# Two graph aggregations by Strassen's seven block products in a four-layer graph kernel on one core

## The reference

```python
x = _layernorm(x + _L0_gnn_ref(...))   # multi-head masked attention, 8 heads
x = _layernorm(x + relu(matmul(matmul(adj, x), W1.T) + b1))
x = _layernorm(x + _L2_gnn_ref(...))   # edge attention
a = adj + eye; d = sum(a, axis=1) ** -0.5
x = _layernorm(x + relu(matmul(d[:, None] * a * d[None, :] @ x, W3.T) + b3))
```

## Time and profile before

| what | us |
|---|---|
| median of 3 runs | 2519.9 (2518.26 to 2522.22) |
| the profiled execution: its own time | 2521.61 |
| the profiled execution: span of its instructions | 2519.8 |
| PE busy in the span | 2411.4 (96%) |
| layer 1: projection, then aggregation | 68.0, then 210.9 |
| layer 3: projection, then aggregation | 67.1, then 210.8 |

### The profile page before, as it was taken

The page is one execution under the profiler, slowest core; times in us unless marked ns, Lnnn a source line. Parts: engine busy times, 40 slices in busy tenths (PEclk is TensorE's granted clock), DMA queues, the critical chain, the costliest instruction groups (busy, mean ns, idle before and its releaser), DMA issues. The chain is left out here.

```text
span 2519.8 us, 66825 instructions
## 1 busy us (share of the span) xinstructions
PE 2411.4 (96%) x24900; PEld 1546.0 (61%) x24900; DVE 1546.1 (61%) x3013; ACT 1364.4 (54%) x2036; POOL 1146.4 (45%) x969
## 2 busy tenths in 40 slices
PE   7998999999999999999799997999999999979998
PEld 6886777777777777777544443774444545434443
DVE  4447888988988988888542223555545566532222
ACT  3337888888888888888533222225343444323221
POOL 0006888888888888888501232001111112310323
PEclk9999999999999999999999998999999999989999
DMA  4228999999999999999543664215668779743564
GB/s 160 67 67 153 191 183 187 195 180 189 195 181 186 195 178 187 194 174 187 103 146 137 213 201 145 90 42 156 172 177 194 194 215 226 167 134 103 207 215 141
DMA packets 783211, 417.40 MB, mean 166 GB/s; under 512 B 691248, under 2 KB 717488, under 8 KB 773936
## 3 DMA queue, kind: packets, MB, share of 16 engines
q1 hardware_dynamic: 783024, 414.62, 71.7%
HBM read 203.55 MB, written 40.84 MB: 97 GB/s over the span
## 5 line engine op out<-in xcount | busy, mean ns | idle before, releaser
L826 DVE CUSTOM_DVE_ANT_0 att_scores<-att_slots,l_bias 128x1024 f32<-128x1024 f32 x528 | 575.9, 1091 | 31.7 <-POOL att_part_low L651 14.2
L651 POOL TENSOR_TENSOR att_part_low<-att_scores,att_part_high 128x1024 f16<-128x1024 f32 x352 | 575.1, 1653 | 11.3 <-ACT att_part_high L810 0.6
L771 ACT ACTIVATE att_scores<-att_scores,att_nmax 128x1024 f32<-128x1024 f32 x528 | 552.4, 1047 | 18.1 <-DVE att_lifted L837 15.8
L692 PE MATMUL att_slots<-l_kk,l_q 128*128 128x512 f16 x2112 | 464.5, 355 | 7.4 <-POOL att_scores L631 4.4
L1365 PE MATMUL a_ps<-l_y,a_adj 128*128 128x512 f16 x1936 | 421.5, 381 | 9.0 <-DVE a_adj L1379 4.7
L780 ACT ACTIVATE att_near_high<-att_ps_t 128x512 f16<-128x512 f32 x528 | 258.2, 524 | 151.6 <-PE att_ps_t L702 138.9
L845 DVE TENSOR_TENSOR att_near_low<-att_ps_t,att_near_high 128x512 f16<-128x512 f32 x528 | 316.4, 599 | 38.5 <-ACT att_near_high L780 36.4
L1365 PEld LDWEIGHTS a_ps<-l_y,a_adj 128*128 128x128 f16 x1936 | 190.0, 98 | 240.5 <-DVE a_adj L1379 5.2
L692 PEld LDWEIGHTS att_slots<-l_kk,l_q 128*128 128x128 f16 x2112 | 194.8, 98 | 163.8 <-DVE att_least L826 20.9
L1110 PE MATMUL edge_ps_o<-l_sup,edge_pt_high 128*128 128x512 f16 x968 | 289.3, 381 | 2.2 <-DMA edge_pt_low<-edge_part_low 2.2
L1350 ACT ACTIVATE a_adj<-l_adj 128x2816 f16<-128x2816 f32 x44 | 112.0, 2549 | 291.0 <-DMA l_adj<-in_adj_cols 270.6
(11 more groups left out here) (157 smaller groups left out, 3836.9 us busy)
## 6 DMA issues: line engine op xcount, KB each, us to landing
l_adj<-in_adj_cols SPq DMA_DIRECT2D x44, 1408.0 KB, 6.1
l_adj_tiles<-in_adj SPq DMA_DIRECT2D x22, 1354.0 KB, 6.0
l_bias<-in_adj SPq DMA_DIRECT2D x63, 384.0 KB, 3.9
p_x_in<-x SPq DMA_DIRECT2D x66, 256.0 KB, 2.6
l_q<-q_rows SPq DMA_DIRECT2D x44, 256.0 KB, 3.9
a_xres<-x SPq DMA_DIRECT2D x44, 256.0 KB, 2.9
p_x_in<-in_x_cols SPq DMA_DIRECT2D x22, 256.0 KB, 2.6
q_rows<-l0w_q_halves SPq DMA_DIRECT2D x22, 256.0 KB, 2.0
```

The lines of the kernel that those rows point to most:

```text
L651: nc.gpsimd.tensor_tensor(out=part[1][:, v, lo:lo + width], in0=sc[:, v, lo:lo + width], in1=part[0][:, v, lo:lo + width], op=ALU.subtract ...
L692: mm = nc.tensor.matmul(slots[:, slot, z:z + w], q[:, u, h % 2, a, h // 2, :], kk[:, h, lo + z:lo + z + w], start=a == 0, stop=a == 1)
L771: nc.scalar.activation(sc[:, v, lo:lo + width], sc[:, v, lo:lo + width], ACT.Exp, bias=nmax[:, v:v + 1], scale=-1.0).then_inc(exp_done, 1)
L826: nc.vector.tensor_tensor_reduce(out=sc[:, v, lo:lo + width], in0=slots[:, (NC * h + c) % 2, 0:width], in1=adj[:, u, lo:lo + width], scale ...
```

## The change

Strassen's form splits adj Y into blocks: rows by odd and even tile of a pair (t = 2m + u), the sum over k by odd and even k, and the 512 columns of Y into two halves. Seven products of sums of blocks take the place of eight, each with 11 k-steps of 256 columns: 7 x 11 x 2 matmuls of 128x256 for a pair of tiles, where there were 2 x 22 x 2 of 128x512.

`project` (layers 1 and 3) now writes seven combinations of Y's blocks: ACT evicts each tile to fp32 (`y32`), and after each odd tile DVE makes five sums, ACT and DVE make the high and low parts of the two plain blocks and of the five sums. ACT narrows adj tiles 0 and 1 at tiles 6 and 10; then SP loads adj tiles 2 and 3; DVE makes the block sums of the first pair at tiles 12 to 15. The loops of `project` in these layers and of `aggregate` are written out.

`aggregate` works by pairs: ACT narrows three pairs deep, DVE makes five block sums of a pair ahead (`combine`), PE seven products, ACT copies four of them out, DVE adds them up in eight steps (`add`), and then bias, residual and statistics for each tile of the pair.

In layer 0 the first rows of adj come in four pieces, each ahead of one of the last four x loads.

```diff
+NARROW_AT = (6, 10)
+SUM_AT = 12
...
+def sum_blocks(nc, blocks, out, n, ready):
+    even, odd = [[blocks[:, u, e::2, :] for u in range(2)] for e in range(2)]
+    if n == 0:
+        for u in range(2):
+            op = nc.vector.tensor_tensor(out=out[:, u, :, :], in0=even[u], in1=odd[u], op=ALU.add)
+    else:
+        a, b, how = ((odd[0], odd[1], ALU.subtract), (even[1], even[0], ALU.subtract), (even[0], odd[1], ALU.add))[n - 1]
+        op = nc.vector.tensor_tensor(out=out[:, 1 + n, :, :], in0=a, in1=b, op=how)
+    op.then_inc(ready, 1)
...
             late(1, 1)
+            more = 0
             for dst, src in prefetch:
                 sp.dma_start(dst, src).then_inc(prefetched, 16)
-            if ahead is not None:
-                sp.dma_start(adj[:, 0, 0:N], adj_rows[0:P, :]).then_inc(first_adj, 16)
-            pairs(sp, 4, T, late)
+            quarters = 0 if ahead is None else len(ADJ_PARTS)
+            if warm is not None:
+                over(sp, 4, NARROW_AT[1] + 3, late)
+                sp.wait_ge(first_narrowed, 2)
+                for t in range(2, 4):
+                    sp.dma_start(a32[:, t % 2, :, :], columns_of(adj_cols, t)).then_inc(prefetched, 16)
+                    more += 1
+                over(sp, NARROW_AT[1] + 3, T, late)
+            else:
+                over(sp, 4, T - quarters, late)
+            for n in range(quarters):
+                lo, width = ADJ_PARTS[n]
+                sp.dma_start(adj[:, 0, lo:lo + width], adj_rows[0:P, lo:lo + width]).then_inc(first_adj, 16)
+                late((T - quarters + n) // 2, (T - quarters + n) % 2)
...
-                        pe.wait_ge(out_low, nj * (2 * m + u - 2) + n + 1)
+                        if combos is None:
+                            pe.wait_ge(out_low, nj * (2 * m + u - 2) + n + 1)
+                        else:
+                            pe.wait_ge(evicted, 2 * m + u - 1)
...
+            def halves(m, u):
+                t = 2 * m + u
+                act.wait_ge(made, t + 1)
+                if m > 1:
+                    act.wait_ge(out_low, 2 * m - 2)
+                scale = V_S * XW if row_scale is None else row_scale[:, bass.ds(t, 1)]
+                slots = y32[:, m % 2, 1::2, :] if u == 0 else y32[:, m % 2, 0::2, :]
+                if t in NARROW_AT:
+                    n = NARROW_AT.index(t)
+                    act.wait_ge(prefetched, 16 * len(prefetch))
+                    nc.scalar.activation(a16[:, 0, n, :, :], a32[:, n, :, :], ACT.Copy).then_inc(first_narrowed, 1)
+                nc.scalar.activation(slots, ps_job[0][:, u, :].rearrange("p (c n) -> p c n", c=2), ACT.Copy,
+                                     scale=scale).then_inc(evicted, 1)
+                if u == 1:
+                    act.wait_ge(evicted, t + 1)
+                    nc.scalar.activation(combos[0][:, 5:7, m, :], y32[:, m % 2, 1:3, :], ACT.Copy).then_inc(out_high, 1)
+                    act.wait_ge(y_summed, 3 * m + 3)
+                    nc.scalar.activation(combos[0][:, 0:5, m, :], sums[:, :, :], ACT.Copy).then_inc(out_high, 1)
...
+            def halves(m, u):
+                if 2 * m + u == SUM_AT:
+                    dve.wait_ge(first_narrowed, 2)
+                    if degrees is not None:
+                        add_identity(nc, a16[:, 0, :, :, :], 0, ident, first_summed)
+                        dve.wait_ge(first_summed, 2)
+                if 0 <= 2 * m + u - SUM_AT < 4:
+                    sum_blocks(nc, a16[:, 0, :, :, :], a_sum[:, 0, :, :, :], 2 * m + u - SUM_AT, first_summed)
+                if u == 0:
+                    return
+                dve.wait_ge(evicted, 2 * m + 2)
+                if m > 0:
+                    dve.wait_ge(out_low, 2 * m)
+                nc.vector.tensor_tensor(out=sums[:, 0:2, :], in0=y32[:, m % 2, 0:2, :], in1=y32[:, m % 2, 2:4, :], op=ALU.add) \
+                    .then_inc(y_summed, 1)
+                nc.vector.tensor_tensor(out=sums[:, 2:4, :], in0=y32[:, m % 2, 0:4:3, :], in1=y32[:, m % 2, 1:3, :],
+                                        op=ALU.subtract).then_inc(y_summed, 1)
+                nc.vector.tensor_tensor(out=sums[:, 4, :], in0=y32[:, m % 2, 1, :], in1=y32[:, m % 2, 2, :], op=ALU.add) \
+                    .then_inc(y_summed, 1)
+                dve.wait_ge(out_high, 2 * m + 1)
+                nc.vector.tensor_tensor(out=combos[1][:, 5:7, m, :], in0=y32[:, m % 2, 1:3, :], in1=combos[0][:, 5:7, m, :],
+                                        op=ALU.subtract).then_inc(out_low, 1)
+                dve.wait_ge(out_high, 2 * m + 2)
+                nc.vector.tensor_tensor(out=combos[1][:, 0:5, m, :], in0=sums[:, :, :], in1=combos[0][:, 0:5, m, :],
+                                        op=ALU.subtract).then_inc(out_low, 1)
...
+            def load_adj(t):
+                if t < T:
+                    sp.wait_ge(narrowed, t - 3)
+                    sp.dma_start(a32[:, t % 2, :, :], columns_of(adj_cols, t)).then_inc(adj_loaded[t % 2], 16)
...
+            for m in range(1, M):
+                load_adj(2 * m + 4)
+                load_adj(2 * m + 5)
+                for u in range(2):
+                    load_x(2 * m + u)
+                    norm.store(sp, out_rows, m - 1, u)
...
+            def narrow(m):
+                for u in range(2):
+                    if m > 1:
+                        act.wait_ge(adj_loaded[u], 16 * (m - 1))
+                    if m > 2:
+                        act.wait_ge(summed, PRODUCTS * (m - 2))
+                    nc.scalar.activation(a16[:, m % 3, u, :, :], a32[:, u, :, :], ACT.Copy).then_inc(narrowed, 1)
+            narrow(1)
+            narrow(2)
+            for m in range(M):
+                for n in range(2):
+                    act.wait_ge(summed, PRODUCTS * m + 2 + 4 * n)
+                    if m > 0:
+                        act.wait_ge(added, ADDS * m)
+                    nc.scalar.activation(copied[:, n, :, :], ps[:, m % 2, 2 * n, :, :], ACT.Copy) \
+                        .then_inc(copies, 1)
+                if m + 3 < M:
+                    narrow(m + 3)
 
...
-            def step(m, u):
-                t = 2 * m + u
-                pe.wait_ge(narrowed if dcol is None else diag_ready, t + 1)
-                if not (isinstance(m, int) and m == 0):
-                    pe.wait_ge(biased, t - 1)
-                for k in range(T):
-                    for b in range(2):
-                        mm = nc.tensor.matmul(ps[:, u, :], a16[:, u, k, :], y[b][:, k, :],
-                                              start=k == 0 and b == 0, stop=k == T - 1 and b == 1)
-                mm.then_inc(summed, 1)
-            step(0, 0)
-            step(0, 1)
-            pairs(pe, 2, T, step)
+            for m in range(M):
+                if m > 0:
+                    pe.wait_ge(combined, 4 * m)
+                if m > 1:
+                    pe.wait_ge(added, ADDS * (m - 1))
+                s16, s2 = a16[:, m % 3, :, :, :], a_sum[:, m % 2, :, :, :]
+                a11, a22 = s16[:, 0, 0::2, :], s16[:, 1, 1::2, :]
+                factors = [(s2[:, 4, :, :], 4), (a22, 2), (s2[:, 0, :, :], 6), (s2[:, 2, :, :], 0),
+                           (a11, 3), (s2[:, 1, :, :], 5), (s2[:, 3, :, :], 1)]
+                for n, (a, c) in enumerate(factors):
+                    for k in range(M):
+                        for b in range(2):
+                            mm = nc.tensor.matmul(ps[:, m % 2, n // 2, n % 2, :], a[:, k, :], y[b][:, c, k, :],
+                                                  start=k == 0 and b == 0, stop=k == M - 1 and b == 1)
+                    mm.then_inc(summed, 1)
 
...
+            def combine(m):
+                s16, out = a16[:, m % 3, :, :, :], a_sum[:, m % 2, :, :, :]
+                dve.wait_ge(narrowed, 2 * m)
+                if dcol is not None:
+                    add_identity(nc, s16, m, ident, diag_ready)
+                    dve.wait_ge(diag_ready, 2 * m)
+                if m > 1:
+                    dve.wait_ge(summed, PRODUCTS * (m - 1))
+                for n in range(4):
+                    sum_blocks(nc, s16, out, n, combined)
+            def add(m):
+                m5, m7, m6 = (ps[:, m % 2, n // 2, n % 2, :] for n in (2, 3, 6))
+                m1, m4, m3, m2 = (copied[:, n // 2, n % 2, :] for n in range(4))
+                c11, c12, c21, c22 = (total[:, n // 2, n % 2, :] for n in range(4))
+                if m > 0:
+                    dve.wait_ge(r_ready, 2 * m)
+                for n, (made, out, a, b, op, own) in enumerate((
+                        (2, c11, m1, m4, ALU.add, 0), (4, c11, c11, m5, ALU.subtract, 1), (4, c11, c11, m7, ALU.add, 2),
+                        (6, c12, m3, m5, ALU.add, 0), (6, c21, m2, m4, ALU.add, 0), (6, c22, m1, m2, ALU.subtract, 0),
+                        (6, c22, c22, m3, ALU.add, 6), (7, c22, c22, m6, ALU.add, 7))):
+                    dve.wait_ge(copies, 2 * m + (1 if made < 6 else 2))
```

(64 more changed lines are left out.)

89 lines of the change are left out of this document (35 added, 54 removed).

## The result

The changed kernel takes 2571.4 us (median of 4 runs, 2568.44 to 2572.69), where the kernel before took 2520.7 beside it: a ratio of 1.0199 (95% interval 1.0186 to 1.0213). It is 50.7 us slower, where 28.6 were forecast; the time lies inside the range given. The profiled execution took 2572.69 us, 51.1 more than that of before.

The account below looks back on a forecast made before the run. PE was taken to bound projections and aggregations. A layer: 33.4 projection + 1.2 front - 24.3 aggregation + 5.5 tail = +15.8; two layers +31.6, layer 0 -3.0: +28.6 us, 2548.5 us; 8-in-10 range 2526 to 2588.

Parts of the forecast that it names:

- The aggregation, -24.3 us a layer: PE in the aggregations: 1694 matmuls of 256 columns at 0.109 us replace 968 of 512, saving 24.3 us a layer.
- rival 2: Aggregations: DVE bounds them, with dear block sums and a POOL normalisation lost per pair; 2587 us, chance 0.09.
- the cheap end: DVE's block sums in the aggregations: about 0.9 us each instead of 1.64, DVE's total 12.8 us a pair instead of 16.5.
- Handover +1.2: Front of the aggregation: the projection's last chain is longer though tile 0's narrowing leaves the gap; 1.2 us more a layer.
- tail +5.5: End of the aggregation: two tiles leave PE at once, 11.3 us to the last normalisation instead of 5.8; 5.5 more a layer.
- layer 0 -3.0: Layer 0: adj rows loaded in four pieces let x 4 come in time, removing PE's idleness of 3.0 us.
- The chain, 2.46 us a pair: Projections: eviction, sums, high and low parts precede DVE's split of tile t+2, so PE waits 2.46 us a pair.
- Rival 1: Projections: PE never waits for DVE's split behind the sums' low part, only for x 13; 2507 us, chance 0.12.
- x of tile 13, 9.8 us: Projections: tile 13's x load queues behind the loads of adj tiles 2 and 3; PE waits 9.8 us a layer.
- rival 4: Projections: x 13 is not late, because small loads pass large ones; 2531 us, chance 0.09.
- The half clock, 1.5 us once a layer: Projections: PE restarts at half clock after 9.8 us of idleness waiting for x 13, losing 1.5 us.
- Rival 3: Projections: PE falls to half clock because it idles in every pair, a pair taking 12.1 us for 8.5; 2613 us, chance 0.05.

Follow-up runs that it names:

- experiment 8: The changed kernel with layer 0's first rows of adj loaded in one piece again, between x tiles 3 and 4: 2571.3 us.
- experiment 1: The changed kernel with ACT's and DVE's high and low parts of a pair moved behind the split of the next tile: 2511.8 us, ratio 0.9968.
- experiment 2: The changed kernel with the loads of adj tiles 2 and 3 moved behind the last x load: 2565.4 us, ratio 1.0177.
- experiment 6: The changed kernel with parts behind the next split and adj loads 2 and 3 behind the last x load, no filler: 2492.0 us, ratio 0.9888.
- Experiments 3 to 5: The changed kernel with unused matmuls before nine products a layer: ten 2548.1 us, five 2546.6, five plus adj loads 2 and 3 last 2532.6.
- experiment 4: The changed kernel with five unused 128x512 matmuls ahead of nine products a layer that wait for the chain: 2546.6 us, ratio 1.0107.
- experiment 5: The changed kernel with the five unused matmuls and the loads of adj tiles 2 and 3 behind the last x load: 2532.6 us, ratio 1.0049.

## Why the prediction was right in direction, and where it fell short

The forecast said slower because the projection would lose more than the aggregation gains, and so it was. By its own steps:

- *The aggregation, -24.3 us a layer.* Measured -23.6 in layer 1 (187.27 for 210.85), 187.3/1694 = 0.110 us a matmul where 0.109 was taken. DVE was no bound, as assumed, and rival 2 is out: its busy time is 121.9 and 127.7 of 187 us. The block sums came out at the cheap end:

```profile
L180 DVE TENSOR_TENSOR l_adj_sum<-l_adj 128x1408 f16<-128x1408 f16 x66 | 58.7, 939 | 0.0
L177 DVE TENSOR_TENSOR l_adj_sum<-l_adj 128x1408 f16<-128x1408 f16 x44 | 37.2, 888 | 6.0 <-ACT l_adj L1469 5.3 <-issue 0.3
```

  Groups by line and form; 1408 elements in 0.89 to 0.94 us, where one result a cycle was put at 1.64. This agrees with the Trainium skill (VectorE: DVE Perf Modes, "The perf-mode tier table"), which gives two 16-bit operands in SBUF twice the rate; the trace of before had shown no such operation.

  The collision with POOL that rival 2 rested on is there, though, and larger than the 0.23 us in the trace of before. POOL's normalisations (min/median/max ns):

```profile
L575 POOL TENSOR_SCALAR a_x_out<-a_residual,a_mv,a_rstd x44: 2080/2082/3610, 1405.0 to 2564.9; 128x512 f32<-128x512 f32 x44
```

  The longest of the 44 before took 2083. Now the 18 that run beside DVE's block sums take 3.56 to 3.61 us, the others 2.1 to 2.3. PE does not feel it (0.1 us of idleness in an aggregation): DVE and POOL (80.2 of 187 us) have the room.
- *Handover +1.2, tail +5.5, layer 0 -3.0.* Measured 5.61 - 4.42 = +1.2 (the 4.25 of the earlier trace rows and the 0.17 by which a matmul's shown length exceeds its own), 11.6 - 5.8 = +5.8, and PE's wait of 3.1 us in layer 0 is gone. Layer 0's last value matmul starts 2.8 us earlier in the trace; experiment 8 gives back 1.6 of it, and the total time could not confirm this term.
- *The chain, 2.46 us a pair.* Measured 42.2/18 = 2.3, and experiment 1, which moves the tail of this chain alone, takes the waits away. Rival 1 is out.
- *x of tile 13, 9.8 us.* Measured 8.07 and 6.27, less than forecast, but the wait is there and experiment 2 takes it away; rival 4 is out.
- *The half clock, 1.5 us once a layer.* **This term failed.** PE's work in the projections took 14.2 us longer in layer 1 and 17.1 in layer 3. The price of one restart was about right: PE's work takes 70.4 us in experiment 1, which keeps only the wait for x of tile 13, and 69.0 in experiment 6, which has neither, 1.4 us apart (2.3 in layer 3). What failed is "once": the forecast let nine waits for the chain pass at full clock. Rival 3 named the mechanism and was dismissed with the sentence that 3.0 us of idleness stayed at 1.00 and so did 8 us in which PE was busy for 4.78. The first row shows a single gap in a stage otherwise full, while the chain makes a gap of some 2.3 us in every pair. The second row stops too early. The next 8 us of the same view of the kernel before have the clock at 0.57:

```profile
1244.00:1252.00 8.00, 5.53 (x15) 1.62 (x13) 1.58 (x3) 0.60 (x1) 0.00 (x0) 0.57 0.00 0
```

  Four waits of 0.7 to 1.8 us had ended between 1234.0 and 1243.7, and a fifth of 1.5 us ran until 1245.8. So the trace of before held a case for rival 3, next to the row that was quoted against it. In experiment 2, with hardly any other wait left inside the projection, the chain's gaps alone cost 18.5 us in layer 1 (86.45 - 67.98).
- *Rival 3's price, 65 us,* was too high: it had PE at half clock for whole pairs. In fact the clock came back after about 3 us, and behind 3 of the 18 waits it did not fall. So the result lies between the forecast and this rival, by the rival's mechanism.

The sum by the trace: projections 42.9 + 45.2, aggregations -23.6 - 23.9, handovers +2.4, tails +11.6, layer 0 -3: +51.6, for 51.1 between the profiled executions. Of the 22 us by which the forecast missed, the half clock makes 28 too few (31.3 for 3.0), and idleness 7 too many (56.9 for 63.8); the second error happened to hide a quarter of the first. Experiments 3 to 5 show that the first is the clock's and not the work's: most of it goes when the waits are shortened to 1.2 us by filler, with the chain as it is.

What is not settled: why one wait of 2.1 to 2.3 us is followed by half clock and the next is not. The rows show both at 1278.69 and 1288.71, with much the same work before them. The length of the wait alone does not decide: lone waits of 2.32, 2.41 and 3.0 us left the clock at full speed, while of the waits of 1.8 to 2.9 us that came in every pair 15 of 18 were followed by half clock, and 20 of 20 in experiment 2. These figures suggest that what went before a wait counts too, but no run varies the distance between waits by itself.

## What to carry to other kernels

Multiplications that fall by an eighth are worth their eighth only if the sums that make this possible do not stand, in an engine's order, ahead of something that the bounding engine waits for. Here a side chain, placed ahead of the split that PE wants next, cost more than both aggregations gave; placed behind it, and with the late loads moved too, the projection took 72.3 us for 68.0. When a change makes the bounding engine wait again and again, price the slower work after the waits as well as the waits; a lone gap of the same length in the trace did not tell here what a train of them would do, and a row quoted against a rival has to be read on into the next one. And when an edit that removes a wait pays less than the wait was long, test it again with the other waits out of the way before calling the wait cheap.

## What the runs showed of the hardware

- TensorE's granted clock went to 0.50 behind 15 of 18 waits of 1.8 to 2.9 us that came back every 8.5 to 10.3 us, and behind all 20 in experiment 2. It stayed at 1.00 around waits of 1.24 to 1.33 us, 8.5 us apart (experiment 4), and behind lone waits of 2.32 and 2.41 us (experiment 5) and of 3.0 us.
- Useless matmuls in the waits made the kernel 23 to 25 us faster.
- POOL's normalisation of 128x512 took 3.56 to 3.61 us beside DVE's two-input fp16 block sums, 2.58 beside DVE's fp32 work on the next tile, and 2.08 with DVE idle.
